# Attention and a mixture-of-experts layer on one core: values kept unsplit in DRAM and split by GpSimd head by head

## The chip, the core and the metric

The kernel runs on one core of a Trainium2 chip. The metric is the device time in microseconds of one execution. The core's engines each follow their own instruction list and meet only at semaphores: TensorE (PE) multiplies, VectorE (DVE), ScalarE (ACT) and GpSimd (POOL) work element by element, SyncE (SP) issues most DMAs. Matrix products are written with fp32r operands. To keep accuracy, an operand is split into a rounded part ("hi") and the rest ("lo"), and products are made with both.

## The reference

```
xn  = layernorm(x)                                   # x: 2 x 1024 x 512
att = softmax(causal(Q K^T / sqrt(32))) V, times Wo  # 16 heads of 32, Q, K, V = xn Wq^T, xn Wk^T, xn Wv^T
ffn = sum over the 2 chosen of 8 experts of w_e * mlp_e(xn) + shared_mlp(xn)
out = x + att + ffn
```

The tokens number 2048, in 16 tiles of 128. There are 2 x 16 = 32 heads of a batch row ("heads" below), each with 1024 queries and keys.

## The kernel before, in words

The work goes through phases: `norm_phase`, `project_phase`, `attend_phase`, `out_phase` and `routed_phase`. Each is a block with one list of instructions per engine, and a phase ends when all its lists have ended.

**norm_phase** (from line 179). Per tile of 128 tokens it loads x, normalizes it, turns it with four transposes, splits the turned tile into `tile_hi` and `tile_lo`, and multiplies by `wv` with twelve products into `ps_v`: that is V. The helper `pipeline(eng, count, unroll, stages, back)` writes each engine's list: at step s it calls, in the order given, each stage (lag, f) for tile s-lag. Four slots are used in turn. The lists are:

- SyncE: `load` (lag 0; line 235; waits until the x slot is normalized), `store_zeros` (0), `store_xn` (3; line 240), `store_v` (5; line 245).
- VectorE: `invert` (1; line 287), `statistics` (0; line 270), `scale` (1; line 294), `lo` (2; line 303), `mean_and_variance` (0; line 276), `split_wv` (2), `v_lo` (4; line 316), `add_eps` (0; line 281), `save_lo` (2; line 309).
- ScalarE: `root` (0; line 348), `hi` (1; line 356), `split_wv` (1), `save_hi` (1; line 361), `v_hi` (3; line 368).
- TensorE: `transpose` (0; line 385), then `multiply` (1; line 396).

V is split here. ScalarE's `v_hi` copies `ps_v` into the first half of each head's 64 columns of `v_stage`, and VectorE's `v_lo` writes `ps_v` less that into the second half. `store_v` waits for `v_lo_ready` and stores 128 x 16 x 64 floats, 512 KB, to `v_dram`. SyncE's list runs in a loop in the middle (`back=0`), the others too.

**project_phase** computes Q and K, the router's logits and the routing. SyncE's first loads there are the bias and a tile of `wqk` (line 476), which ScalarE splits first (line 526).

**attend_phase** (from line 743). One list of steps is written out for all engines: 32 heads of NB = 12 blocks, one block (a stretch of up to 512 queries by 128 keys) a step. Each stage has a lag: the row maxima run 24 steps (`AHEAD`) ahead of the scores (line 1433), exp (line 1213) has lag 24, `hi` 25 (line 1220), `lo` 26, the products with V `VALUE` = 30 (lines 1456 and 1458). `lo` (prob_lo, the rest of the probabilities) is made by GpSimd (line 1175) for ten blocks of a head and by VectorE for n = 4 and 8 (line 1302). The widths of a head's blocks n = 0 to 11 are 512, 256, 384, 128, 512, 256, 512, 384, 512, 128, 512 and 512. There are 4 buffers of `prob`, so exp of step s waits for the `lo` of step s-4. A fixed number of the shared MLP's products (lines 1489 and 1514) is put into each step of TensorE by `fill_counts`, from costs written in the code.

GpSimd's list has one `lo` per step and, after it, one step of `placing_steps`, the routing: 48 of them ahead of step 0, the last 32 being indirect DMAs to `slots_dram` (line 1145).

VectorE's `normalize` and `weigh_o` (lines 1327 and 1331) finish half a head's output. TensorE's `turn_row` (line 1420), once per head, waits for the L1331 of the half before.

SyncE's list goes by heads g: `load_head(g)` (six DMAs, lines 958 and 960, which wait until the scores of head g-4 are done), at certain g `load_xt`, `store_acc` and `load_base`, then `load_values(g - 1)` (line 967), then raw shared weights. `load_values` fetches 128 x 8 x 64 floats, 256 KB, in pieces of 256 bytes, into `vs`, which has four slots (`HS`) and is read directly as the stationary operand of the V products; it waits until head g-4 has been multiplied (`pv_done`). The last two columns of a slot are ones.

## Time and profile before

| | |
|---|---|
| median of 3 runs | 1165.86 us (1165.05 to 1168.9) |
| the profiled execution, its own time | 1170.92 us |
| its span, first to last instruction | 1169.1 us |
| mean granted TensorE clock | 0.963 of full speed |
| TensorE, VectorE, ScalarE, GpSimd busy | 1055.6, 769.1, 647.0, 505.2 us |
| norm_phase | about 0 to 70.8 us |
| project_phase | to about 183 us |
| attend_phase | to about 780 us |
| out_phase and routed_phase | the rest |

A row of a group gives the line, the engine, the operation, the tile written and the tile read, the shape and the count, then the busy time and the mean of one in ns, then the idle time of the engine just ahead of them and what ended it. A row of a timeline gives the start and the duration in us first; instructions of one kind that follow one another are merged into one row with their count. "SPq" and "ACTq" are the sequencers that issue DMAs.

### The profile page before, as it was taken

How to read it: one execution, taken by the hardware profiler on the slowest of the kernel's cores; microseconds unless marked ns; L12 is line 12 of the kernel's file. 1: busy time of each engine (PE TensorE's matmuls, PEld its weight loads, DVE VectorE, ACT ScalarE, POOL GpSimd, SP SyncE). 2: the span in 40 equal slices, each digit the busy share in tenths (PEclk: the TensorE clock that was granted, in tenths of full speed). 3: DMA queues.
4: the chain of work that ended last, by engine and by line, in shares of the span. 5: the costliest groups of instructions: out<-in, count | busy, mean ns of one | idle time of the engine just before them, and what ended most of it. 6: DMA issues, size and time to landing. Idle time of an engine off the chain costs nothing. (4 is left out here: it accounts for less than half of the span.)

```text
span 1169.1 us, 19196 instructions
## 1 busy us (share of the span) xinstructions
PE 1055.6 (90%) x5379; PEld 819.2 (70%) x5380; DVE 769.1 (66%) x1729; ACT 647.0 (55%) x1291; POOL 505.2 (43%) x566
## 2 busy tenths in 40 slices
PE   5979995978999999999999999989879999999994
PEld 4857873756677776777777777757668777777773
DVE  6832344646578878877777777555367777777782
ACT  4523220445677777777787777851155555555551
POOL 0001815389656555555655565540013333334331
PEclk9989996989899999999999999989989999999998
DMA  5987978578145265444343444038793334433332
GB/s 190 316 320 294 153 268 264 107 119 152 37 145 145 53 202 99 146 115 146 100 112 116 145 133 130 2 119 284 234 370 64 66 72 72 72 65 66 71 69 36
DMA packets 109559, 165.68 MB, mean 142 GB/s; under 512 B 54016, under 2 KB 64512, under 8 KB 106272
## 3 DMA queue, kind: packets, MB, share of 16 engines
q1 hardware_dynamic: 99136, 143.92, 43.0%
q0 software_dynamic: 9760, 20.49, 9.9%
q8 instruction: 37, 0.61, 0.2%
q14 instruction: 50, 0.41, 0.1%
q10 hardware_dynamic: 576, 0.26, 0.1%
HBM read 103.35 MB, written 61.28 MB: 141 GB/s over the span
## 5 line engine op out<-in xcount | busy, mean ns | idle before, releaser
L1175 POOL TENSOR_TENSOR prob_lo<-prob,prob_hi 128x512 fp32r<-128x512 f32 (+2 forms) x320 | 308.2, 977 | 224.2 <-ACT prob_hi L1220 169.4
L1213 ACT ACTIVATE prob<-ps_s 128x512 f32<-128x512 f32 (+3 forms) x384 | 188.2, 490 | 141.1 <-PE ps_s L1438 95.9
L1220 ACT ACTIVATE prob_hi<-prob 128x512 fp32r<-128x512 f32 (+3 forms) x384 | 198.5, 517 | 12.7 <-ACT row_stage L1194 12.7
L1283 DVE CUSTOM_DVE_ANT_0 ps_m<-ps_m,causal 128x384 f32<-128x384 f32 (+3 forms) x256 | 126.8, 496 | 75.2 <-PE ps_m L1409 74.1
L1851 DVE TENSOR_TENSOR rw_lo<-gu_sb,rw_hi 128x704 fp32r<-128x704 f32 x156 | 138.9, 893 | 48.9 <-ACT rw_hi L1786 44.3
L1765 POOL DMA_INDIRECT out<-work,rows x39 | 61.6, 1580 | 251.6 <-DVE rows L1812 131.5
L1409 PE MATMUL ps_m<-ks,qs 96*128 96x512 f32 (+3 forms) x384 | 140.0, 366 | 13.8 <-DMA ks<-qk_hi 12.8
L1786 ACT ACTIVATE rw_hi<-gu_sb 128x704 fp32r x156 | 123.4, 793 | 47.9 <-PE ps_ru L1884 32.4
L1433 PE MATMUL ps_s<-qs,ks 97*128 97x512 f32 (+3 forms) x384 | 138.3, 360 | 2.7 <-ACT prob L1213 2.6
L1456 PE MATMUL ps_o<-prob_hi,vs 128*66 128x512 f32 (+3 forms) x384 | 132.1, 344 | 9.3 <-issue 5.3
L1287 DVE TENSOR_REDUCE maxima<-ps_m 128x1 f32<-128x512 f32 x128 | 86.8, 686 | 69.2 <-PE ps_m L1409 68.8
L1458 PE MATMUL ps_o<-prob_lo,vs 128*66 128x512 f32 (+3 forms) x384 | 130.7, 341 | 0.0
L1905 PE MATMUL ps_ry<-d_sb,work 128*128 (+1 forms) x234 | 106.9, 592 | 1.2 <-issue 1.2
L1409 PEld LDWEIGHTS ps_m<-ks,qs 96*128 96x128 f32 x384 | 75.0, 196 | 36.6 <-issue 13.6
L1433 PEld LDWEIGHTS ps_s<-qs,ks 97*128 97x128 f32 x384 | 73.9, 193 | 18.4 <-ACT prob L1213 4.6
L1489 PE MATMUL ps_f<-xt,sg_hi 128*128 128x512 f32 (+1 forms) x192 | 73.0, 414 | 4.6 <-DMA xt<-xt_blocks 4.6
L1456 PEld LDWEIGHTS ps_o<-prob_hi,vs 128*66 128x66 f32 x384 | 53.6, 140 | 29.2 <-issue 13.8
L1777 ACT ACTIVATE xg_hi<-ps_xt 128x512 fp32r<-128x512 f32 x39 | 23.3, 598 | 91.3 <-PE ps_xt L1872 91.3
L1905 PEld LDWEIGHTS ps_ry<-d_sb,work 128*128 128x128 f32 (+1 forms) x234 | 43.1, 189 | 38.8 <-issue 38.8
L1489 PE MATMUL ps_f<-xt,su_hi 128*128 128x512 f32 (+1 forms) x192 | 70.3, 400 | 0.0
L1438 PE MATMUL ps_s<-late,eye 128*128 128x128 f32 x256 | 61.0, 238 | 0.0
L689 DVE TENSOR_TENSOR work<-ps_q,work 128x512 fp32r<-128x512 f32 x32 | 21.8, 690 | 58.8 <-ACT work L537 56.8
(211 smaller groups left out, 2416.2 us busy)
## 6 DMA issues: line engine op xcount, KB each, us to landing
xt<-xt_blocks SPq DMA_DIRECT2D x8, 2048.0 KB, 8.5
v_rows<-work SPq DMA_DIRECT2D x16, 512.0 KB, 2.9
qk_hi<-work SPq DMA_DIRECT2D x8, 1024.0 KB, 4.1
qk_lo<-work SPq DMA_DIRECT2D x8, 1024.0 KB, 7.0
qs<-qk_hi SPq DMA_DIRECT2D x64, 128.0 KB, 2.9
ks<-qk_hi SPq DMA_DIRECT2D x64, 128.0 KB, 3.1
vs<-v_rows SPq DMA_DIRECT2D x32, 256.0 KB, 5.0
out<-y_acc SPq DMA_DIRECT2D x32, 256.0 KB, 3.5
```

What stands on the lines that cost most here:

```text
L1175: nc.gpsimd.tensor_tensor(prob_lo[:, s % NPL, 0:w], prob[:, s % NP, 0:w], prob_hi[:, s % NPH, 0:w].bitcast(F32), ALU.subtract).then_inc(lo ...
L1213: nc.scalar.activation(prob[:, s % NP, 0:w], ps_s[s % NS][:, 0:w], ACT.Exp, scale=SCALE).then_inc(exp_done, 1)
L1220: nc.scalar.activation(prob_hi[:, s % NPH, 0:w], prob[:, s % NP, 0:w], ACT.Copy).then_inc(hi_ready, 1)
L1283: nc.vector.tensor_tensor_reduce(ps_m[s % NM][:, 0:w], ps_m[s % NM][:, 0:w], causal[:, TBW - w:], 1.0, MASKED, ALU.add, ALU.max, maxima[:, ...
L1409: nc.tensor.matmul(ps_m[s % NM][:, 0:w], qs[0:ROWS, c, t * P:(t + 1) * P], ks[0:ROWS, c, k0:k0 + w], start=True, stop=True).then_inc(m_don ...
L1433: last = nc.tensor.matmul(ps_s[s % NS][:, 0:w], ks[0:ROWS + 1, c, kt * P:(kt + 1) * P], qs[0:ROWS + 1, c, q0:q0 + w], start=True, stop=not ...
L1456: nc.tensor.matmul(into, vs[:, c, kt, :], prob_hi[:, s % NPH, 0:w], start=n in STARTS, stop=False)
L1458: nc.tensor.matmul(into, vs[:, c, kt, :], prob_lo[:, s % NPL, 0:w], start=False, stop=n in ENDS).then_inc(pv_done, 1)
L1489: last = nc.tensor.matmul(ps_f[part][0:w, :], (w_hi, w_lo, w_hi)[term][:, kc, f0:f0 + w], xt[:, (0, 0, 1)[term], kc, :], start=(j == 0), s ...
L1786: nc.scalar.activation(w_hi[:, k, :], chunk(e, k), ACT.Copy).then_inc(w_hi_ready, 1)
L1851: nc.vector.tensor_tensor(w_lo[:, k, :], chunk(e, k), w_hi[:, k, :].bitcast(F32), ALU.subtract).then_inc(w_lo_ready, 1)
L1905: last = nc.tensor.matmul(ps_y[c % 2][:, :], hid_t[0:w, c % HR, k, :], d_sb[0:w, bass.ds(e * NF + k, 1), :].rearrange("p a d -> p (a d)"), ...
```

## The change

V is stored whole: `v_dram` has 32 columns per head, ScalarE copies `ps_v` in one piece, `v_lo` on VectorE is gone, and `store_v` (now 256 KB, lag 4, all steps of SyncE written out) waits for ScalarE. In `attend_phase`, `load_values` goes to one buffer `v_raw` (128 KB in pieces of 128 bytes) two heads behind `load_head` instead of one, and waits until the head before has been split. GpSimd's list gets `split_values` behind `lo`, at the step at which a head's scores begin and the next one: a copy of 128 x 256 into the hi columns of `vs`, then a subtraction of 128 x 256 into the lo columns. TensorE waits for `values_split` instead of the load.

```diff
@@ -87,7 +87,7 @@
...
     qk_lo = nc.dram_tensor("qk_lo", [2 * D, T], F32, kind="Internal").ap()
-    v_dram = nc.dram_tensor("v_rows", [P, NT, H, 2 * DK], F32, kind="Internal").ap()
+    v_dram = nc.dram_tensor("v_rows", [P, NT, H, DK], F32, kind="Internal").ap()
     row_dram = nc.dram_tensor("max_rows", [2 * H, S], F32, kind="Internal").ap()
...
@@ -188,7 +188,7 @@
...
         rstd = sbuf("rstd", [P, U])
-        v_rows = U * H * 2 * DK // D
+        v_rows = U * H * DK // D
         xn = work[:, v_rows:v_rows + U, :]
...
@@ -197,8 +197,7 @@
...
         wv_lo = sbuf("wv_lo", [P, KC, D], F32R)
-        v_stage = work[:, 0:v_rows, :].bitcast(F32R).rearrange(
-            "p (u a) (h d) -> p u (a h) d", u=U, d=2 * DK)
+        v_stage = work[:, 0:v_rows, :]
         ps_t = [psum(f"ps_t{n}", [P, KC, P]) for n in range(U)]
...
@@ -220,8 +219,7 @@
...
         r_loaded = sem("r_loaded")
-        v_hi_ready = sem("v_hi_ready")
-        v_lo_ready = sem("v_lo_ready")
+        v_ready = sem("v_ready")
         zeros_ready = sem("zeros_ready")
...
@@ -241,9 +239,9 @@
...
                     t = U * i + c
-                    wait(sp, v_lo_ready, t + 1)
-                    sp.dma_start(v_dram[:, bass.ds(t, 1)].rearrange("p a h d -> p (a h) d"),
-                                 v_stage[:, c].bitcast(F32)).then_inc(v_stored[c], 16)
+                    wait(sp, v_ready, t + 1)
+                    sp.dma_start(v_dram[:, bass.ds(t, 1)].rearrange("p a h d -> p (a h d)"),
+                                 v_stage[:, c, :]).then_inc(v_stored[c], 16)
...
@@ -253,7 +251,8 @@
...
-                pipeline(sp, NT, U, [(0, load), (0, store_zeros), (3, store_xn), (5, store_v)])
+                pipeline(sp, NT, U, [(0, load), (0, store_zeros), (3, store_xn), (4, store_v)],
+                         back=NT)
...
@@ -309,14 +308,6 @@
...
-                def v_lo(i, c):
-                    t = U * i + c
-                    wait(dve, v_hi_ready, t + 1)
-                    v = v_stage[:, c]
-                    nc.vector.tensor_tensor(v[:, :, DK:], ps_v[c][:, :].rearrange("p (h d) -> p h d", h=H),
-                                            v[:, :, 0:DK].bitcast(F32),
-                                            ALU.subtract).then_inc(v_lo_ready, 1)
-
                 nc.vector.memset(zeros, 0.0).then_inc(zeros_ready, 1)
...
@@ -327,7 +318,7 @@
...
                     (1, invert), (0, statistics), (1, scale), (2, lo), (0, mean_and_variance),
-                    (2, split_wv), (4, v_lo), (0, add_eps), (2, save_lo)], back=U)
+                    (2, split_wv), (0, add_eps), (2, save_lo)], back=U)
...
@@ -361,15 +352,13 @@
...
-                def v_hi(i, c):
+                def save_v(i, c):
                     t = U * i + c
...
                     wait(act, v_stored[c], 16 * i)
-                    nc.scalar.activation(v_stage[:, c, :, 0:DK],
-                                         ps_v[c][:, :].rearrange("p (h d) -> p h d", h=H),
-                                         ACT.Copy).then_inc(v_hi_ready, 1)
-
-                pipeline(act, NT, U, [(0, root), (1, hi), (1, split_wv), (1, save_hi), (3, v_hi)])
+                    nc.scalar.activation(v_stage[:, c, :], ps_v[c][:, :], ACT.Copy).then_inc(v_ready, 1)
+
+                pipeline(act, NT, U, [(0, root), (1, hi), (1, split_wv), (1, save_hi), (3, save_v)])
                 act.wait_ge(r_loaded, 16)
...
@@ -389,7 +378,7 @@
...
                     wait(pe, lo_ready, t + 1)
-                    wait(pe, v_lo_ready, t - U + 1)
+                    wait(pe, v_ready, t - U + 1)
                     n = 0
...
@@ -844,6 +833,7 @@
...
         ks = sbuf("ks", [P, HS, S], F32R)
+        v_raw = sbuf("v_raw", [P, QT, DK])
         vs = sbuf("vs", [P, HS, QT, VW], F32R)
...
@@ -892,7 +882,8 @@
...
         head_loaded = [sem(f"head_loaded{n}") for n in range(HS)]
-        values_loaded = [sem(f"values_loaded{n}") for n in range(HS)]
+        values_loaded = sem("values_loaded")
+        values_split = sem("values_split")
         row_saved = sem("row_saved")
...
@@ -962,10 +953,10 @@
...
                 def load_values(g):
-                    c, h, b = g % HS, g // B, g % B
-                    wait(sp, pv_done, NB * (g - HS + 1))
-                    sp.dma_start(vs[:, c, :, 0:2 * DK].bitcast(F32),
-                                 v_dram[:, b * QT:(b + 1) * QT, h, :]).then_inc(values_loaded[c], 16)
+                    h, b = g // B, g % B
+                    wait(sp, values_split, 2 * g)
+                    sp.dma_start(v_raw[:, :, :], v_dram[:, b * QT:(b + 1) * QT, h]
+                                 ).then_inc(values_loaded, 16)
...
@@ -1017,8 +1008,8 @@
...
                             load_base(unit)
-                    if 0 < g <= HEADS:
-                        load_values(g - 1)
+                    if 2 <= g < HEADS + 2:
+                        load_values(g - 2)
                     for k in range(NF):
...
@@ -1177,9 +1168,22 @@
...
+                def split_values(s):
+                    g, c = s // NB, s // NB % HS
+                    if s % NB == 0:
+                        pool.wait_ge(values_loaded, 16 * (g + 1))
+                        wait(pool, pv_done, NB * (g - HS + 1))
+                        nc.gpsimd.tensor_copy(vs[:, c, :, 0:DK], v_raw[:, :, :]
+                                              ).then_inc(values_split, 1)
+                    if s % NB == 1:
+                        pool.wait_ge(values_split, 2 * g + 1)
+                        nc.gpsimd.tensor_tensor(vs[:, c, :, DK:2 * DK], v_raw[:, :, :],
+                                                vs[:, c, :, 0:DK].bitcast(F32),
+                                                ALU.subtract).then_inc(values_split, 1)
+
                 for _ in range(48):
                     next(placing_steps, None)
-                steps([(LO, lo)])
+                steps([(LO, lo), (AHEAD, split_values)])
                 for _ in placing_steps:
...
@@ -1445,7 +1449,7 @@
...
                     if n == 0:
-                        pe.wait_ge(values_loaded[c], 16 * (g // HS + 1))
+                        pe.wait_ge(values_split, 2 * (g + 1))
                     if n in STARTS:
...
```

## Rows read from the trace of the kernel before

**Rows 1.** The page, busy time, share of the span and instructions of an engine.

```profile
PE 1055.6 (90%) x5379; PEld 819.2 (70%) x5380; DVE 769.1 (66%) x1729; ACT 647.0 (55%) x1291; POOL 505.2 (43%) x566
```

**Rows 2.** Busy time of the engines by stretch, then clock, DMA share and GB/s.

```profile
240.00:273.00 33.00, 25.04 (x114) 19.18 (x114) 16.99 (x42) 15.59 (x37) 29.72 (x30) 0.84 0.78 152
...
306.00:339.00 33.00, 31.81 (x181) 25.02 (x180) 25.22 (x72) 25.86 (x58) 18.95 (x20) 1.00 0.46 129
```

**Rows 3.** Timeline of norm_phase, tiles 4 to 6 and 14.

```profile
26.40 0.60 PE L385 MATMUL ps_t<-ident,work 128*128 128x128 f32 x4
...
27.17 0.60 ACT L356 ACTIVATE tile_hi<-ps_t 128x512 fp32r<-128x512 f32 x1 [0.49 <-PE ps_t L385]
...
28.43 0.58 ACT L368 ACTIVATE work<-ps_v 128x512 fp32r<-128x512 f32 x1
...
30.44 0.69 DVE L270 BATCH_NORM_STATS2 stats<-x_tile 128x6 f32<-128x512 f32 x1 [0.21 <-DMA x_tile<-in_x]
...
31.05 0.53 DVE L294 TENSOR_SCALAR work<-x_tile,moments,rstd 128x512 f32<-128x512 f32 x1
...
32.87 0.14 DVE L281 TENSOR_SCALAR var_eps<-moments 128x1 f32<-128x1 f32 x1
...
58.95 0.60 PE L385 MATMUL ps_t<-ident,work 128*128 128x128 f32 x4
```

**Rows 4.** Timeline of the end of norm_phase, VectorE.

```profile
69.02 0.69 DVE L316 TENSOR_TENSOR work<-ps_v,work 128x512 fp32r<-128x512 f32 x1 [2.08 <-ACT work L368]
```

**Rows 5.** Waits from 222 to 300 us, and GpSimd's timeline at 295 us.

```profile
ACT prob L1213 <- POOL prob_lo L1175: 21.1, 18, 1.7
...
295.36 0.99 POOL L1145 DMA_INDIRECT slots<-entry,slot_of  x1 [0.17 <-issue]
```

**Rows 6.** TensorE's L1420 and VectorE's L1331, then timelines of two heads.

```profile
  DVE work L1331: 20.9, 28
...
L1331 DVE TENSOR_TENSOR work<-o_sum,o_inv x64: 291/338/1694, 239.3 to 779.8; 128x128 f32<-128x128 f32 x64
...
407.64 4.51 POOL L1175 TENSOR_TENSOR prob_lo<-prob,prob_hi 128x512 fp32r<-128x512 f32 x4 [1.03 <-ACT prob_hi L1220]
...
410.95 0.61 DVE L1331 TENSOR_TENSOR work<-o_sum,o_inv 128x128 f32<-128x128 f32 x1
...
676.56 1.29 POOL L1175 TENSOR_TENSOR prob_lo<-prob,prob_hi 128x512 fp32r<-128x512 f32 x1 [1.03 <-ACT prob_hi L1220]
...
678.08 3.51 POOL L1175 TENSOR_TENSOR prob_lo<-prob,prob_hi 128x512 fp32r<-128x512 f32 x3 [0.24 <-ACT prob_hi L1220]
...
680.16 0.84 DVE L1331 TENSOR_TENSOR work<-o_sum,o_inv 128x128 f32<-128x128 f32 x1
```

**Rows 7.** Timeline of SyncE's issues in norm_phase.

```profile
23.07 0.33 SPq L245 DMA_DIRECT2D v_rows<-work  x1
...
23.45 0.43 SPq L235 DMA_DIRECT2D x_tile<-in_x  x1
```

**Rows 8.** DMA issues near 23 and 16 us, then x loads' landings.

```profile
v_rows<-work SPq DMA_DIRECT2D x1, 512.0 KB, 2.9
...
x_tile<-in_x SPq DMA_DIRECT2D x1, 256.0 KB, 3.4
...
xn_rows<-work SPq DMA_DIRECT2D x1, 256.0 KB, 2.0
...
DMA to landing us min/median/max: 2.7/3.5/8.1
```

**Rows 9.** Groups of GpSimd by form.

```profile
L1175 POOL TENSOR_TENSOR prob_lo<-prob,prob_hi 128x256 fp32r<-128x256 f32 x64 | 48.2, 753 | 61.4 <-ACT prob_hi L1220 57.6 <-PE ps_o L1458 3.7
...
L662 POOL CAST sg_hi<-sg_raw 128x1408 fp32r<-128x1408 f32 x1 | 1.4, 1372 | 0.0
...
L669 POOL CAST sd_hi<-sd_raw 128x1024 fp32r<-128x1024 f32 x1 | 1.1, 1052 | 0.0
```

**Rows 10.** The page's DMA issues: count, KB each, median us to landing.

```profile
vs<-v_rows SPq DMA_DIRECT2D x32, 256.0 KB, 5.0
```

## The prediction

> **What bounds the kernel now.** I read the page first. TensorE is busy for 90% of the span [rows 1], so it is the engine to watch, but the mean hides three stretches that the change touches, and each has its own limit. The busy time by stretch shows two of them: from 306 us on TensorE is busy for 31.8 of 33 us while GpSimd has 19.0, but from 240 to 273 us GpSimd is busy for 29.7 of 33 us and TensorE for only 25.0 [rows 2].
>
> The first stretch, norm_phase, needs the timelines. TensorE's transposes start at 26.40 us for tile 4 and at 58.95 us for tile 14 [rows 3]: 32.55 us for ten tiles, 3.26 each. Inside it TensorE is busy throughout, so VectorE's `v_lo` (0.69 us, 16 times [rows 4]) lies beside it. What nearly ends last is a loop through SyncE: a load of x is queued behind a store of V, and the store waits until V is copied out.
>
> The end of the phase is a plain chain: ScalarE's copy, VectorE's `v_lo`, the last issue, the block's end, then the first w_raw load of the next phase. `v_lo` of tile 15, at 69.02 us, is the last of VectorE's work there [rows 4].
>
> In attention, ScalarE's exp waits 21.1 us in all for GpSimd's prob_lo between 222 and 300 us, and the last of the 32 routing DMAs on GpSimd starts at 295.36 us [rows 5]. Until then GpSimd sets the pace, afterwards TensorE does. In the later part TensorE stops once per head at `turn_row`, for L1331 on VectorE: 20.9 us over 28 heads [rows 6].
>
> **Norm phase: the SyncE queue.** `store_v` moves from lag 5 to lag 4. Before, the load of tile s+1 stood behind the store of V tile s-5; now it stands behind that of s-4. The first load that met a V store was that of tile 6 (store at 23.07, load at 23.45 us) [rows 7]. Now it is that of tile 5. V tile 0 is copied out one `v_lo` before its store, at 23.07-0.69 = 22.38 us at the latest; one issue (23.45-23.07 = 0.38 us) later load 5 goes, at 22.73 us.
>
> Call L the time from a load's issue to its landing. Statistics of tile 5 start at 22.73+L. From statistics to the end of scale there are 31.05+0.53-30.44 = 1.14 us [rows 3], and with an estimated 0.13 us of signalling the transpose starts 1.27 us after statistics. Tile 4's transpose is then at 24.00+L, against 26.40: a shift of L-2.40.
>
> The loop after that: the `root` of the next tile stands ahead of ScalarE's `hi`. VectorE reaches add_eps 32.87-30.44 = 2.43 us after statistics; without `v_lo` in front of it, about 0.6 us sooner. Root and signalling add an estimated 0.4, so `hi` starts at 2.2 us; V's copy ends 28.43+0.58-27.17 = 1.84 us after `hi` starts [rows 3]; store and next load take 0.41. So 4.45+L us after statistics of tile k+1 those of tile k+3 can start: two tiles in 4.45+L against 6.51 before. Over tiles 4 to 14 that is five times L-2.06. Together the phase grows by 6L-12.7.
>
> L is the large unknown. With a 512 KB store just ahead it was 3.4 us; that store alone landed in 2.9, a lone 256 KB store in 2.0, the quickest load of x in 2.7 [rows 8]. Taking the stores' slope (0.9 us for 256 KB) off 3.4 gives 2.5, the lower bound; the upper is 3.1, 2.7 for a load plus what is left of the smaller store. I take 2.75, since the quickest load is the nearest row. The phase then grows by 6 x 2.75 - 12.7 = **+3.8 us** (2.3 to 5.9).
>
> The Trainium skill (DMA: Bandwidth & Descriptors, Anatomy of one DMA) gives about 2.0 us fixed plus the bytes at 436 GB/s. For 512 KB of V and x behind one another that is an estimate of 3.2 us from the store's issue, L = 2.8, and the phase would grow by 4.1 us by it. Our own lone store of 2.0 us is already quicker than its 2.6.
>
> **The phase's end.** The last `v_lo` (0.69 us) was on the path [rows 4]: **-0.7 us**. The first w_raw load stood behind a 512 KB store and now behind 256 KB; between nothing and the 0.9 us that separates the two stores [rows 8], I take **-0.4 us**. The router's r_lo moves up with it. ScalarE's copy keeps its 512 elements: nothing. Unrolling SyncE's loop saves only sequencing on a queue that mostly waits: nothing beyond what L covers.
>
> **Attention: two more GpSimd instructions per head.** The subtraction of 256 elements is the form 128x256 of prob_lo, 0.753 us. The copy goes by the two CASTs, 1.372 us for 1408 elements and 1.052 for 1024: slope 0.83 ns, so 0.41 us for 256 [rows 9]. Consecutive GpSimd instructions overlap by about 0.05 us (four of them, 512, 512, 512 and 256 wide, take 4.51 us [rows 6]), so a head adds 0.36+0.70+0.04 of waits = 1.1 us. No row shows the copy's strided write; it could cost nothing or half as much again.
>
> Head 0's split comes before the first prob_lo, where GpSimd idles: nothing. Those of heads 1, 2 and 3 fall between 240 and 296 us, where GpSimd sets the pace: 3 x 1.1 = **+3.3 us** (2.0 if waits elsewhere swallow one, 4.8 if strides cost). TensorE does not win it back, because its filling work is fixed per step.
>
> The other 28 splits fall between prob_lo of n = 10 and 11 and between 11 and 0. ScalarE's exp four steps on needs these; its margin is about one us, so the delay is hidden. If that cover goes, each head costs up to 1.1 us.
>
> But the order on GpSimd also sets when L1331 is let through. VectorE's L1331 is ready at 410.95, takes 0.61 us where the quickest takes 0.29, and ends just after GpSimd's third 512 (407.64 + 3 x 1.26 = 411.4); TensorE goes on at once [rows 6]. Afterwards GpSimd's instruction boundaries lie at 1.26, 1.6, 2.9, 3.65 and 4.9 us from the group's start instead of 1.26, 2.5, 3.8. L1331, ready at 3.31, is let through at 3.65 instead of 3.8. In some later heads ScalarE delays the second 512 (678.08 us in the group of 676.56 us): L1331, ready at 3.60, ends only at 4.4 [rows 6]. There the copy fills the gap and some 0.3 is won. 28 x 0.1 is 2.8 us. The bounds are -5 and, with slow strides, +3; I take **-2.5 us**.
>
> Value loads halve in bytes and come a head later. SyncE now waits in `load_values` for the split of the head before, some 4 us per head; behind it stand only raw weights that are needed much later and the next `load_head`, which waits longer anyway. A value load landed in a median of 5.0 us [rows 10], and has about twelve steps of 1.4 us, less those 4: hidden.
>
> **Sum:** 3.8-0.7-0.4+3.3-2.5 = +3.5 us. The profiled execution took 1170.92 us (span 1169.1 and 1.8 around it), 5.1 above the median of 1165.86. Added to its own time that is 1174.4; against the median, 1169.4. I give the latter.
>
> **Rivals.**
> - *No loop in norm_phase.* If L drops to 2.1, like the lone store, the phase stays at TensorE's pace: +3.5-3.8 gives about -0.3 us, 1165.6. For: the traffic per tile falls by a quarter. Against: no x load landed in under 2.7.
> - *L1331 slips in a boundary earlier* (the faster side). After the change a boundary lies near 2.9 us from the group's start. L1331 is ready at 3.1 (the least of the 28 heads) to 3.6. If copy and waits take 0.2 to 0.4 us longer than I think, the boundary reaches it in over half of the heads and TensorE's stop of about 0.6 us is gone there: 18 x 0.6 = 10.8 us off; with the other terms (+6) it ends at about 1161. It decides at a boundary later than 3.1 us. The Trainium skill (SBUF — State Buffer, Who interferes with whom) says that a VectorE instruction with two SBUF inputs and a GpSimd instruction that reads SBUF exclude each other for the whole instruction, whoever starts first; by it any boundary serves, and the trace agrees (0.61 against 0.29 us).
> - *L1331 slips past the subtraction.* If it becomes ready after 3.65 us, it waits for the third 512 until 4.9: +1.1 us a head, for ten heads 11 us: 1180. Its readiness reached 3.6, so this is close.
> - *A value load late.* If a base load ahead of it delays one past its split, GpSimd stops for one to three us in a few heads: 1172 to 1175.
>
> **Chances.** Forecast 0.45, no loop 0.2, L1331 earlier 0.15, L1331 later 0.12, late values 0.08. A measurement of this kernel tells about 0.3% (3.5 us) from no change. My forecast lies on that edge, so half of its chance is "same"; the no-loop case is "same"; both late cases are "slower"; L1331 earlier is "faster". Faster 0.16, same 0.41, slower 0.43. The forecast's own bounds, all low or all high, are -2 and +13 (1164 to 1179); with the earlier L1331 taken in and the rarest of the late ends left out the range is 1161 to 1178.
>
> **What would show it.** Transposes in norm_phase 3.5 to 3.7 us apart with short TensorE gaps, waiting on VectorE and x; the first projection product some 3 us later than before; two GpSimd rows of about 0.4 and 0.75 us, 32 times each; the last routing DMA about 6 us later; the stop at `turn_row` slightly under 0.75 us a head. I am wrong if the transposes stay 3.26 us apart, or if turn_row's stop in total moves by more than 5 us.

## The result, and the profile after

The changed kernel is slower: 1180.8 us in the median of 15 runs (1170.37 to 1185.67) against 1162.55 us for 15 runs of the kernel before (1154.81 to 1168.9). The ratio of the means is 1.0132, 95% interval 1.0104 to 1.0161, or 15.4 us (12.1 to 18.7); the medians lie 18.3 us apart. The forecast was 1169.4, its range ended at 1178, and the least likely rival but one (chance 0.12) had said 1180. All of these were counted from 1165.86 us, the median of three runs; as differences the forecast was +3.5 us and the end of its range +12. The profiled execution took 1183.31 us with a span of 1180.7.

The table places the difference by milestones of TensorE, each number a mean of three profiled executions of one kernel, in us (lines are those of before; after's are in brackets).

| stretch on TensorE | before | after | difference |
|---|---|---|---|
| start to the first product of projection, L577 (L566) | 76.0 | 80.4 | +4.4 |
| from there to the first product of attention, L1409 (L1413) | 117.1 | 121.0 | +3.9 |
| to `turn_row` of head 0, L1420 (L1424) | 14.4 | 13.6 | -0.7 |
| `turn_row` of head 0 to that of head 5 | 104.5 | 106.5 | +2.0 |
| head 5 to head 15 | 168.0 | 165.2 | -2.8 |
| head 15 to head 24 | 149.9 | 158.9 | +9.05 |
| head 24 to the last product of attention | 147.7 | 146.0 | -1.6 |
| from there to the end of the span | 388.7 | 387.3 | -1.4 |

Five terms matter: the norm phase, the projection phase, the first heads, and two of opposite sign in the heads that follow. Of these, +9.05 repeats to 0.1 us in all three profiles; +3.9 does not (117.9, 121.7 and 123.4 us after, 116.9 to 117.4 before). The -1.4 is no effect that could be told from chance: the same stretch differs by 3.5 us among the three profiles of before. The whole table adds up to 12.8 us, the difference of the mean spans.

The page's line of busy time:

```profile
PE 1060.9 (90%) x5379; PEld 820.4 (69%) x5380; DVE 762.7 (65%) x1713; ACT 647.8 (55%) x1291; POOL 537.8 (46%) x630
```

Busy time by stretch, columns as in [rows 2], the second stretch holding the ends of heads 16 and 17:

```profile
240.00:273.00 33.00, 27.04 (x138) 20.82 (x137) 19.73 (x53) 16.92 (x39) 29.60 (x31) 0.90 0.75 107
...
500.00:533.00 33.00, 29.37 (x167) 22.92 (x167) 26.77 (x65) 24.46 (x55) 20.26 (x23) 1.00 0.44 120
```

Against [rows 1], GpSimd has 32.6 us and 64 instructions more, VectorE 6.4 us and 16 fewer. From 240 to 273 us GpSimd is as full as in [rows 2]. From 500 to 533 us it has room for 12 us, and yet TensorE is busy 2.4 us less than in the steady stretch of before.

What the split costs stands in the groups of GpSimd by form:

```profile
L1180 POOL TENSOR_TENSOR vs<-v_raw,vs 128x256 fp32r<-128x256 f32 x32 | 23.0, 720 | 0.2
L1176 POOL CAST vs<-v_raw 128x256 fp32r<-128x256 f32 x32 | 14.4, 450 | 4.8 <-DMA v_raw<-v_rows 4.7
```

In the steady heads the two take 0.69 and 0.40 us; the means hold a few that ran beside VectorE. The estimate had 0.753 and 0.41. All of the idle time is one wait, before the first head: value loads are on time.

Norm phase, two of the longest waits up to 72 us (what waits for what: us, times, longest):

```profile
DVE stats L269 <- DMA x_tile<-in_x: 18.7, 12, 3.3
PE ps_t L374 <- DVE work L293: 11.2, 8, 6.5
```

Timelines of the same phase, the transposes of tiles 4 and 14 and two of SyncE's issues:

```profile
25.68 0.54 PE L374 MATMUL ps_t<-ident,work 128*128 128x128 f32 x3 [0.59 <-DVE work L293]
...
63.83 0.65 PE L374 MATMUL ps_t<-ident,work 128*128 128x128 f32 x4
...
24.21 0.32 SPq L243 DMA_DIRECT2D v_rows<-work  x1
24.57 0.43 SPq L233 DMA_DIRECT2D x_tile<-in_x  x1
```

Ten tiles take 38.15 us instead of the 32.55 of [rows 3], and VectorE waits 18.7 us for x in all, three times the 6.0 us of before. The load of x is issued right after the store of V that it stands behind, 0.36 us later: the loop through SyncE is there.

Now the steady heads. VectorE's product `work<-o_sum,o_inv`, L1331 in [rows 6], is L1335 here. The timelines of GpSimd, VectorE and TensorE at the end of head 16, the first of the nine long ones:

```profile
501.55 1.29 POOL L1166 TENSOR_TENSOR prob_lo<-prob,prob_hi 128x512 fp32r<-128x512 f32 x1 [1.07 <-ACT prob_hi L1224]
502.79 0.40 POOL L1176 CAST vs<-v_raw 128x256 fp32r<-128x256 f32 x1
503.15 1.29 POOL L1166 TENSOR_TENSOR prob_lo<-prob,prob_hi 128x512 fp32r<-128x512 f32 x1
504.40 0.69 POOL L1180 TENSOR_TENSOR vs<-v_raw,vs 128x256 fp32r<-128x256 f32 x1
505.06 1.25 POOL L1166 TENSOR_TENSOR prob_lo<-prob,prob_hi 128x512 fp32r<-128x512 f32 x1
...
505.16 1.30 DVE L1335 TENSOR_TENSOR work<-o_sum,o_inv 128x128 f32<-128x128 f32 x1
...
506.61 0.27 PE L1424 MATMUL ps_x<-ident,maxima 128*8 128x128 f32 x1 [1.57 <-DVE work L1335]
```

GpSimd's group starts at 501.55. Its next instructions start 1.24, 1.60, 2.85 and 3.51 us later. L1335 becomes ready 3.61 us after the start, 0.10 us after the subtraction has given way to the third 512, and takes 1.30 us, to just past the end of that instruction. TensorE stands for 1.57 us. In heads 5 to 15 L1335 is ready while the subtraction still runs, takes 0.36 to 0.40 us in eight of the eleven heads and about 0.6 in three, and TensorE stands for 0.14 to 0.39 us instead of about 0.6 before. That is the -2.8 and -1.6 of the table, and the nine long heads (16 to 24, stops of 1.35 to 2.05 us) are the +9.05.

What ended TensorE's idle time before L1424, to be set beside the first row of [rows 6]:

```profile
  DVE work L1335: 22.3, 25
```

The sum hides the matter: 22.3 us after 20.9, since short stops got shorter and nine got long. Only the stops head by head show it.

### The profile page after: what moved, and what is told of

It reads as the page before. It is cut to its first block and busy times, and to the rows that moved or that the text cites. A ratio compares the mean times of both kernels' runs of the same rounds, so it can differ in the third digit from the quotient of the medians.

```text
span 1180.7 us, 19201 instructions
## 1 busy us (share of the span) xinstructions
PE 1060.9 (90%) x5379; PEld 820.4 (69%) x5380; DVE 762.7 (65%) x1713; ACT 647.8 (55%) x1291; POOL 537.8 (46%) x630
## 5 line engine op out<-in xcount | busy, mean ns | idle before, releaser
L1413 PE MATMUL ps_m<-ks,qs 96*128 96x512 f32 (+3 forms) x384 | 140.6, 368 | 13.7 <-DMA ks<-qk_hi 12.8
L1790 ACT ACTIVATE rw_hi<-gu_sb 128x704 fp32r x156 | 123.5, 793 | 48.7 <-PE ps_ru L1888 33.8
L1413 PEld LDWEIGHTS ps_m<-ks,qs 96*128 96x128 f32 x384 | 75.2, 196 | 36.7 <-issue 13.7
L1437 PEld LDWEIGHTS ps_s<-qs,ks 97*128 97x128 f32 x384 | 74.2, 193 | 26.4 <-ACT prob L1217 10.4
L1460 PEld LDWEIGHTS ps_o<-prob_hi,vs 128*66 128x66 f32 x384 | 53.9, 140 | 28.2 <-issue 14.6
L566 PE MATMUL ps_q<-xt_hi,w_hi 128*128 128x512 f32 x128 | 52.0, 406 | 12.1 <-DVE w_lo L668 6.6
```

What stands on the lines that cost most here:

```text
L1413: nc.tensor.matmul(ps_m[s % NM][:, 0:w], qs[0:ROWS, c, t * P:(t + 1) * P], ks[0:ROWS, c, k0:k0 + w], start=True, stop=True).then_inc(m_don ...
L1437: last = nc.tensor.matmul(ps_s[s % NS][:, 0:w], ks[0:ROWS + 1, c, kt * P:(kt + 1) * P], qs[0:ROWS + 1, c, q0:q0 + w], start=True, stop=not ...
L1460: nc.tensor.matmul(into, vs[:, c, kt, :], prob_hi[:, s % NPH, 0:w], start=n in STARTS, stop=False)
L1790: nc.scalar.activation(w_hi[:, k, :], chunk(e, k), ACT.Copy).then_inc(w_hi_ready, 1)
```

## The experiments

Times are set against the kernel before on the same chip. "Stretch" is the time from the first product of projection to the first of attention.

| kernel | ratio to before, 95% interval | first projection product | stretch | heads 0 to 5 | heads 15 to 24 |
|---|---|---|---|---|---|
| a1_lag5 | 1.0096 (1.0059 to 1.0133) | 73.81 | 121.2 | 106.3 | 158.9 |
| a2_late_split | 1.0073 (1.0043 to 1.0103) | 80.26 | 120.3 | 106.6 | 149.9 |
| a3_norm_only | 1.0072 (1.0048 to 1.0097) | 79.68 | 123.3 | 104.0 | 149.8 |
| a4_attn_only | 1.0043 (1.0022 to 1.0064) | 75.66 | 117.6 | 106.7 | 159.0 |
| b3_lag5_late | 1.0003 (0.9975 to 1.0031) | 73.96 | 123.1 | 106.6 | 149.9 |
| b4_longer | 1.0088 (1.0055 to 1.0121) | 80.15 | 123.1 | 107.0 | 149.4 |
| c1_same_place | 1.0019 (0.9995 to 1.0042) | 72.56 | 118.0 | 105.7 | 149.9 |
| c2_looped | 1.0007 (0.9987 to 1.0027) | 75.02 | 115.7 | 106.7 | 149.9 |
| c3_spread | 1.0019 (0.9995 to 1.0042) | 73.02 | 120.8 | 95.3 | 149.9 |
| c4_pads_act | 1.0011 (0.9989 to 1.0034) | 74.29 | 116.7 | 106.7 | 149.9 |
| d1_same_place | 1.0093 (1.0057 to 1.0129) | 78.61 | 117.8 | 106.0 | 159.0 |
| d3_after_again | 1.0107 (1.0059 to 1.0154) | 79.86 | 117.9 | 106.8 | 159.0 |
| d4_slots | 0.9909 (0.9878 to 0.9941) | 73.25 | 122.7 | 89.2 | 149.8 |
| e1_before_slots | 0.9879 (0.9841 to 0.9917) | 76.19 | 116.9 | 89.4 | 149.9 |
| e2_four_slots | 1.0104 (1.0050 to 1.0158) | 73.45 | 123.5 | 97.5 | 149.9 |

**One part at a time.** a1_lag5, from the changed kernel:

```diff
-pipeline(sp, NT, U, [(0, load), (0, store_zeros), (3, store_xn), (4, store_v)],
+pipeline(sp, NT, U, [(0, load), (0, store_zeros), (3, store_xn), (5, store_v)],
          back=NT)
```

> The changed kernel with `store_v` back at lag 5 in SyncE's order of norm_phase; V is still stored whole, 256 KB a tile. Theory (the queue loop costs the norm phase its 3.5 us): load s+1 again stands behind the store of tile s-5, the transposes of tiles 4 to 14 are again 3.2 to 3.3 us apart instead of 3.8, and the first projection product starts at 75 to 76.5 us instead of 79.99. Attention keeps its shape: about nine heads with a stop of 1.3 to 2.1 us at turn_row. Time 3.5 to 4.5 us under the changed kernel, ratio to before about 1.010. Rival (the norm phase is slower for another reason, such as what the smaller stores do to the DMA traffic): the transposes stay 3.8 us apart and the product near 80 us.

The first projection product came at 73.81 us, 6 us earlier than in the changed kernel and 2 us earlier than before: lag 4 is the whole loss of the norm phase, whose transposes are 3.2 us apart again. What makes it quicker than before (the missing `v_lo`, the smaller stores, SyncE's list written out) was not separated. VectorE's wait for x fell from 18.7 us to 3.7. The nine heads stayed.

a2_late_split, from the changed kernel:

```diff
 def split_values(s):
...
-    if s % NB == 0:
+    if s % NB == 2:
...
-    if s % NB == 1:
+    if s % NB == 3:
...
```

> The changed kernel with GpSimd's split moved by two steps: the copy comes after prob_lo of n = 0 and the subtraction after that of n = 1, so that around `weigh_o` (the product that VectorE does before turn_row) GpSimd's instruction boundaries are again those of before. The amount of work is the same. Theory (a late `weigh_o` slips past the subtraction): the stops at turn_row of 1.3 to 2.1 us in heads 16 to 24 go back to 0.6 to 0.9, the stretch from turn_row of head 15 to that of head 24 takes about 150 us instead of 159, time 8 to 10 us under the changed kernel, at or below before's plus 3. Rival A (GpSimd simply has too much work, 1.1 us a head more): the stretch stays at 155 us or more wherever the split stands. Rival B (the longer stretch comes from later value loads or another wait): the same.

The theory held to 0.1 us: heads 15 to 24 take 149.9 us. At head 16 GpSimd runs both 512s in one piece, and L1335, ready 3.61 us after the start of the group as in the changed kernel, takes 0.33 us:

```profile
502.75 2.53 POOL L1166 TENSOR_TENSOR prob_lo<-prob,prob_hi 128x512 fp32r<-128x512 f32 x2
...
505.10 0.33 DVE L1335 TENSOR_TENSOR work<-o_sum,o_inv 128x128 f32<-128x128 f32 x1
```

The amount of work is the same, so rival A falls; so does B. The size was expected too large (8 to 10 us under the changed kernel, at most 3 over before): 8.5 us are left over before, 7 fewer than the changed kernel's 15.4. With the nine long stops the gain of the other heads went too (about 0.6 us of stop again in each), and the long stretch stayed.

a3_norm_only and a4_attn_only exchange the two halves, each with the edits of the diff in one phase alone. Both leave out the lower part of V in the products: a3 loads whole values straight into the first half of `vs` and sets the second half to zero, a4 splits values that have no lower part left.

> The norm phase of the changed kernel (V stored whole, lag 4) with the attention of before: no split on GpSimd, the value load goes straight into the place that the products read, and only into its first half, in pieces of 128 bytes; the second half is set to zero once. It leaves out the lower part of V in the products; the number and shapes of the products are kept. Theory: norm phase as in the changed kernel (first projection product at 79 to 80.5 us, +3.5), attention as before (turn_row to turn_row of heads 15 to 24 about 150 us, no stop above 1 us, GpSimd-paced heads 1 to 3 without the extra 2.4 us); ratio to before 1.003. If the extra 6 us between the first projection product and the first attention product belong to the change, they are seen here again; if they are chance of the transfers, they are seen in some of these kernels and not in others. Rival (the norm phase's delay shifts what comes later and so makes the slow heads): stops of 1.3 us or more in heads 16 to 24 here too, ratio 1.010 or more.

> The norm phase of before (V split there, stores of 512 KB, lag 5) with the attention of the changed kernel: GpSimd splits a head's values, loaded from the first halves alone. It leaves out the lower part of V, which comes out as zero; all instructions of the attention are there. Theory: first projection product at 76 to 77 us as before; attention as in the changed kernel, with some nine heads of 1.3 to 2.1 us at turn_row, +2.4 us in heads 1 to 3; ratio to before 1.006 to 1.010. With a3_norm_only the two excesses should add up to that of the changed kernel (1.013). Rival (the slow heads need the norm phase's delay as well): no stop above 1 us, ratio under 1.004.

Both theories held in where the time goes, the nine long stops in a4 alone, but neither ratio was met: a3 came to 1.0072 instead of 1.003, a4 to 1.0043 instead of 1.006 to 1.010. The excesses, 0.72 and 0.43%, add up to 1.15%, inside the interval of the changed kernel. Of a3's 8 us only 3 to 4 come from the norm phase; its profiled execution had a stretch of 123.3 us, 6 more than before, which the prediction had not priced. In a4, with split stores, the stretch stayed at 117.6.

**More work, less time.** b4_longer, from the changed kernel:

```diff
+spare = sbuf("spare", [P, 2, DK])
...
 nc.gpsimd.tensor_copy(vs[:, c, :, 0:DK], v_raw[:, :, :]
                       ).then_inc(values_split, 1)
+nc.gpsimd.tensor_copy(spare[:, :, :], v_raw[:, 0:2, :])
```

> The changed kernel with more work: GpSimd copies another 128x128 elements to a place that nobody reads, right after its copy of the split, some 0.3 us a head. Theory (`weigh_o` misses the end of the subtraction by 0.1 us and is then shut out for a whole 512 instruction): the subtraction now ends 0.3 us later, `weigh_o` becomes ready inside it in all heads, the nine long stops of 1.4 to 2.1 us shrink to 0.5 to 0.8, the others grow from 0.37 to about 0.65; heads 15 to 24 take about 151 us instead of 159 and the kernel gets 2 to 6 us faster by doing more, although heads 1 to 3, which GpSimd paces, lose 1 us. Rival (GpSimd has too much work per head, or the stops come from something else): nothing is gained, and each head is 0.3 us longer or the same; time 0 to 10 us above the changed kernel.

The size given there is a slip: the copy is 128x64. Head 16 again:

```profile
502.53 1.30 POOL L1167 TENSOR_TENSOR prob_lo<-prob,prob_hi 128x512 fp32r<-128x512 f32 x1 [1.07 <-ACT prob_hi L1226]
503.78 0.40 POOL L1177 CAST vs<-v_raw 128x256 fp32r<-128x256 f32 x1
504.12 0.23 POOL L1179 COPY spare<-v_raw 128x64 f32<-128x64 f32 x1
504.32 1.29 POOL L1167 TENSOR_TENSOR prob_lo<-prob,prob_hi 128x512 fp32r<-128x512 f32 x1
505.56 0.69 POOL L1182 TENSOR_TENSOR vs<-v_raw,vs 128x256 fp32r<-128x256 f32 x1
...
506.15 0.29 DVE L1337 TENSOR_TENSOR work<-o_sum,o_inv 128x128 f32<-128x128 f32 x1
```

The product is ready 3.62 us after the group's start, the same as in the changed kernel, but the subtraction now ends at 3.72, so that the product is let in as soon as it ends and takes 0.29 us. Eight of the nine long stops are gone (head 19, ready later, keeps 2.22 us); heads 15 to 24 take 149.4 us instead of 158.9. GpSimd does 0.2 us a head more, and yet from its first to its last product attention takes 583.6 us against 589.4 to 591.0 in the three profiles of the changed kernel. In the whole time the gain is within the intervals: 1.0088 beside 1.0132 and 1.0107 of the changed kernel.

**The two repairs together**, b3_lag5_late (both diffs above):

> The changed kernel with both repairs: `store_v` back at lag 5 and the split two steps later on GpSimd. Theory (the two costs are separate and add up): first projection product at 74 us (2.5 us before that of before), attention as in a2_late_split (no stop above 1.2 us, heads 1 to 3 still 2.4 us longer in all); ratio to before 0.998 to 1.004. Rival (they are not separate, or the smaller stores cost elsewhere, between projection and attention): 1.006 or more.

The time is that of before, 1.0003. Its profiled execution, the slowest of its twelve runs, shows the long stretch all the same (123.1), so that stretch may vary from run to run.

**The stretch in the projection phase.** Repeats, and two possible causes:

> The changed kernel once more, unchanged: how much of its profile repeats? The nine heads with a stop of 1.3 to 2.1 us (heads 16 to 24) are set by the order of instructions and should be there again, the stretch of heads 15 to 24 at 159 us again, and the transposes of norm_phase about 3.8 us apart again. Left open by the first four runs: the 3 to 6 us between the first projection product and the first attention product (123.4 us in the changed kernel, 117.4 in before). Theory (it comes with the whole stores of V): 120 us or more again. Rival (chance of the transfers): 117 to 119 us here.

> The kernel before once more, unchanged, for the same question: from the first projection product to the first attention product 117 to 118 us if that stretch is fixed by the kernel, 119 to 123 us here if it is chance. Stops at turn_row again 0.6 to 1.2 us in every head, 20.9 us in all; first projection product at 76 us.

They gave 121.7 and 116.9 us. In the phase ScalarE waits for the seventh load of w_raw, which stands on SyncE's queue behind the store of the routing table's pads, 39 KB in pieces of 8 bytes. That wait in the timeline of before, and then in that of the changed kernel:

```profile
156.79 0.63 ACT L526 ACTIVATE w_hi<-w_raw 128x512 fp32r<-128x512 f32 x1 [10.15 <-DMA w_raw<-in_wqk]
```

```profile
163.71 0.63 ACT L515 ACTIVATE w_hi<-w_raw 128x512 fp32r<-128x512 f32 x1 [14.55 <-DMA w_raw<-in_wqk]
```

The pads in the changed kernel's DMA issues (KB, us from issue to landing; 23.3 before):

```profile
slots<-slot_table SPq DMA_DIRECT2D x1, 39.0 KB, 27.3
```

In the ten profiles with a long stretch (120 us or more) ScalarE waited 12.0 to 14.6 us for this load, in the ten others 9.4 to 11.6. TensorE runs dry in the wait, and its granted clock from 150 to 180 us was 0.89 to 0.94 in the ten long ones and 1.00 in the others. So a longer wait is paid twice.

c1_same_place (from b3_lag5_late) and d1_same_place (from the changed kernel):

```diff
-v_dram = nc.dram_tensor("v_rows", [P, NT, H, DK], F32, kind="Internal").ap()
+v_dram = nc.dram_tensor("v_rows", [2, P, NT, H, DK], F32, kind="Internal").ap()[0]
```

> b3_lag5_late (V stored whole, lag 5, late split), with the tensor of V in HBM declared as large as before and only its first half used, so that every tensor behind it, the slot table's among them, is at the address that it had before. What is open: from the first projection product to the first attention product it took 116.9 to 117.6 us in the three profiles with split stores of V and 120.3 to 123.4 us in the seven with whole ones, and the store of the pads to the slot table took 23.3 to 24.0 against 24.9 to 27.3 us. Theory (the address of the slot table decides how fast its 4992 small writes go): pads in 23 to 24 us, the stretch back at 117 to 118 us. Rival (it comes from the order or the size of DMAs in norm_phase): 120 us or more again, pads 25 us or more.

c2_looped is b3_lag5_late without `back=NT`, so that SyncE's list runs in its loop again:

> b3_lag5_late with SyncE's order of norm_phase in its loop again instead of written out in full (`back=NT` taken away). Theory (addresses): nothing changes, the stretch from the first projection product to the first attention product stays at 120 to 123.5 us. Rival (the unrolled issues of the norm phase leave the queue in another state for the small writes that follow): back at 117 to 118 us. The norm phase itself: transposes 3.2 to 3.3 us apart as in b3_lag5_late, first projection product within 0.5 us of 74.

118.0 and 115.7 us: each met the number of the theory or rival that the other refutes, so this pair decides nothing. On the next chip:

> The changed kernel with the tensor of V declared as large as before and its first half used, so that the addresses of the tensors behind it are those of before; nothing else differs from d3_after_again, on the same chip. Theory (the address of the slot table makes its small writes slower): from the first projection product to the first attention product 117 to 118.5 us here and 120 to 123.5 in d3_after_again; time 4 us less. Rival (timing left behind by the norm phase at lag 4): 120 us or more in both, times within 2 us.

> The changed kernel once more, on the same chip as d1_same_place and timed with it. From the first projection product to the first attention product 120 to 123.5 us by both theories, the nine locked heads again; ratio to before about 1.013.

> The kernel before once more, beside the other two on the same chip. From the first projection product to the first attention product 116.5 to 118 us by both theories; 119 or more would say that chance alone can lengthen this stretch.

117.8, 117.9 and 116.9 us. The changed kernel itself can have the short stretch, and d4_slots and e2_four_slots, with the old addresses, had 122.7 and 123.5: the address theory falls. What remains is a count, over several chips. With split stores of V all five profiles had 116.9 to 117.6 us; with whole ones ten of fifteen had 120.3 to 123.5, the rest 115.7 to 118.0. The cause stays open, chance included.

**The pads from another queue.** c4_pads_act moves `store_pads` from SyncE's order to ScalarE's, at the same step, in b3_lag5_late:

> b3_lag5_late with the store of the pads (39 KB in pieces of 8 bytes) issued from ScalarE's queue instead of SyncE's, at the same step. Theory (the load of w_raw waits 10 to 14 us because it stands behind these pieces in one queue, and TensorE's clock falls in the stop that follows): the wait for w_raw falls under 3 us, TensorE does not stop, and the stretch from the first projection product to the first attention product takes 110 to 115 us instead of 123; 5 to 12 us faster than b3_lag5_late. Rival (the small pieces fill the 16 DMA engines whatever queue they come from): the wait stays at 8 us or more, time unchanged.

ScalarE still waited 10.3 us for w_raw. The small pieces hold up the load from either queue. While they run, the engines are busy and move nearly nothing (a window of the kernel before, columns as in [rows 2]; the DMA share is above 1 where the times of packets overlap):

```profile
135.00:140.00 5.00, 5.00 (x24) 4.14 (x23) 2.59 (x3) 1.72 (x3) 4.85 (x4) 1.00 1.93 2
```

**The first heads.** c3_spread adds two empty steps after each routing DMA in b3_lag5_late:

```diff
...
     entry[:, t, k, :], None).then_inc(entries_stored, 16)
 yield
+yield
+yield
...
```

> b3_lag5_late with the 32 routing DMAs of GpSimd spread over every third step of attention instead of every step. Theory (heads 1 to 5 are paced by GpSimd alone, at 17 to 28 us a head against 16.6 later, and the split's 2.4 us are lost there): heads 1 to 5 come down to under 20 us each, the split costs nothing more there, and the kernel is 8 to 20 us faster than b3_lag5_late, so faster than before. Rival (these heads are paced by VectorE or by late loads of xt, GpSimd only looks busy): turn_row of head 5 no more than 3 us earlier. A DMA standing between prob_lo steps in more heads can shut `weigh_o` out there: one or two stops above 1.3 us are possible.

Heads 0 to 5 took 95.3 us instead of 106.6, but TensorE stood 2.1 to 3.4 us at `turn_row` in heads 2 to 9, and at head 9 nothing was left of it. A DMA now stood between the 512s, and the product waited through it, through the next 512 and through the copy of the split behind that. Head 6:

```profile
317.47 0.99 POOL L1136 DMA_INDIRECT slots<-entry,slot_of  x1
318.49 1.27 POOL L1168 TENSOR_TENSOR prob_lo<-prob,prob_hi 128x512 fp32r<-128x512 f32 x1
319.69 0.41 POOL L1178 CAST vs<-v_raw 128x256 fp32r<-128x256 f32 x1
...
317.85 2.40 DVE L1337 TENSOR_TENSOR work<-o_sum,o_inv 128x128 f32<-128x128 f32 x1
```

The copy ends at 320.10 us and the product at 320.25. In head 9 it waited through the DMA and four instructions more, 3.64 us. Where the product became ready beside a `prob_lo` or a subtraction, as in the heads above, it was let in at the next boundary; why it was not after a DMA, no run shows.

So the DMAs were put into steps far from it. d4_slots, from c1_same_place, with a list `routing_now` that is empty until the DMAs begin:

```diff
+routing_now.append(1)
 for t in range(NT):
...
-next(placing_steps, None)
+if not routing_now or n in (4, 6, 8):
+    next(placing_steps, None)
```

> c1_same_place with the 32 routing DMAs of GpSimd placed only at the steps n = 4, 6 and 8 of a head (three a head), far from the steps in which VectorE's product for turn_row is made. Theory (heads 1 to 5 are paced by GpSimd's total of work, and c3_spread's stops of 2.2 us came from a DMA between prob_lo of n = 10 and 0, which moved GpSimd's boundaries): heads 2 to 10 take 16.5 to 18 us each without stops above 1.2 us, turn_row of head 10 comes 15 to 20 us earlier than in c1_same_place (391.61 there), and the kernel is 10 to 20 us faster than before, ratio about 0.985. Rival (something else, such as the late first load of xt or the fill given to those steps, holds heads 1 to 5): head 10 no more than 5 us earlier.

It beats both kernels: 1156.08 us, ratio 0.9909. Heads 0 to 5 take 89.2 us, head 10 comes 12 us earlier after head 0 than in c1 (15 to 20 were expected); two heads of 20 us are left (2 and 10), and ahead of the second a value load came 4.6 us late. The same placing without the change, and four DMAs a head:

> The kernel before with one edit: the 32 routing DMAs of GpSimd only at the steps n = 4, 6 and 8 of a head, as in d4_slots; V split in norm_phase as before. Theory (the split costs what it adds to a GpSimd that has no room, and nothing once it has): head 10 as early after head 0 as in d4_slots within 2 us (155.4 us there from turn_row of head 0 to that of head 9), time within 3 us of d4_slots, 10 us under before. Rival (the split costs 2.4 us in heads 1 to 3 whatever else stands there): 3 to 6 us under d4_slots.

> d4_slots with four DMAs a head, at n = 4, 5, 7 and 8. Theory (three a head leave GpSimd time to spare, and the twelfth head's waits come from the DMAs ending late): they end three heads earlier and the two long heads around head 10 (20.3 us) come down to 17, 2 to 4 us faster than d4_slots. Rival (four a head fill GpSimd: 9.4 us of prob_lo, 1.1 of the split and 4.6 of DMAs in 16.3 us): heads 2 to 9 grow to 18 us or more, and it is slower than d4_slots by 5 us or more.

e1 (that edit alone in the kernel before) took 1153.49 us, 0.9879; head 9 comes 155.55 us after head 0 against 155.40 in d4: with room on GpSimd these two profiles show no cost of the split there, and the intervals of the two ratios overlap. e2 lost what d4 had won, 1.0104. Four a head make GpSimd the pace again, heads 2 to 9 take 19 to 22 us. Head 10, which was to come down from 20.3 us to 17, came down to 18.7.

## Why the prediction was wrong, by its steps

**Queue loop in norm_phase: right in mechanism, too small.** Predicted +3.8 us and transposes 3.5 to 3.7 us apart; ten tiles took 5.6 us more, 3.8 apart, where the prediction's period made it 3.5 us more. The term mis-sized is L, taken from the quickest load (2.75 us); the median landing in the changed kernel is 3.1, and the loop's period, 4.45+L for two tiles, gives L = 3.2 for the measured 7.63. The first term, a shift of tile 4's transpose by L-2.40 = 0.35 us, can't be tested: that transpose starts at 25.1 to 26.4 us in the three profiles of before and at 25.7 to 27.2 in those of after. At tile 14 the phase is 4.9 us late in the first pair of profiles and 5.9 in the means, inside the bounds of 2.3 to 5.9. The figure (2.0 us and 436 GB/s) that the prediction took from the Trainium skill (DMA: Bandwidth & Descriptors, Anatomy of one DMA) is a fit for DMAs that GpSimd issues; these are SyncE's. a1_lag5 showed that the lag alone does it. The end of the phase (-1.1) held: from tile 14's transpose to the first projection product it is 1.35 us shorter (17.51 to 16.16).

**Projection phase: not in the prediction.** +3.9 us in the mean of three. The pads were never looked at, although the wait of 10.15 us is in the trace of before. a3_norm_only, with the change in the norm phase alone, had it (123.3 us), but no run showed that the change causes it.

**First heads: right, a little large.** Predicted +3.3 us, measured +2.0 (+2.4 in the first pair of profiles); the last routing DMA starts at 306.95 us instead of 295.36 [rows 5], 2.1 us more than attention itself starts later.

**The term of -2.5 us for the order on GpSimd: this step failed.** It came out at +4.65 us. It said that L1331, "ready at 3.31, is let through at 3.65 instead of 3.8". Two numbers of it were wrong together. The subtraction gives way at 3.51 us, not 3.65: it starts at 2.85 instead of 2.9 and takes 0.69 us, with the overlap 0.66, instead of the 0.753 of prob_lo. And ready at 3.31 is true of one group of heads: in the trace of before L1331 is ready at 3.60 to 3.62 us (once 3.92) in heads 16 to 24, at 3.06 to 3.32 in heads 5 to 15. Heads 26 to 28 are at 3.60 too, but there ScalarE holds up the second 512 and with it the boundaries; the one head of 3.60 in [rows 6] is of that kind, and the text says "reached 3.6", without a count. With 0.05 us between 3.60 and 3.65 even the predicted boundaries left the sign of the term open for nine heads at once. The heads outside the nine gave -4.4 us, near the favourable bound of -5; the nine gave +9.05.

**The rival.** *L1331 slips past the subtraction* had the place, the price (1.1 us a head against 1.0) and the number of heads (ten against nine). Its stated point of decision, 3.65 us, was the faulty number. That its 1180 us met the measured median is in part luck: it held nothing for the projection phase (+3.9) and kept the -2.5 us, and it started from a median 3.3 us above that of the 15 runs. The Trainium skill (SBUF — State Buffer, Who interferes with whom) says that a VectorE instruction with two SBUF inputs contends with a GpSimd instruction that reads SBUF, and that the one issued later is blocked; the trace agrees, 1.30 us for L1335 beside a 512 of 1.25 that started 0.10 us ahead of it. b4_longer shows that the boundary decides: moved 0.2 us later it undid eight of nine.

**The test named for it was blunt.** It would be wrong "if turn_row's stop in total moves by more than 5 us": it moved by 1.4.

**Hidden parts.** Value loads and SyncE's new waits were hidden, as said: one wait of 4.7 us, before the first head.

**The sum.** The steps of attention and norm give 4.4+2.0-2.8+9.05-1.6 = 11.1 us, and the projection's 3.9 makes 15.0. With the two small stretches that no step explains (-0.7 and -1.4) the profiled executions differ by 12.8 us, near the lower end of the 12.1 to 18.7 measured over 15 runs each.

## What to carry to other kernels

Where two engines shut each other out of SBUF, what counts is at which instruction boundary the waiting one becomes ready, not how busy either is. List its readiness for every iteration against the boundaries as they will be; if one group lies within a tenth of a microsecond of a boundary, price both sides by their count. Put added work on such an engine where nobody waits for it, and look there first for work that already stands in the wrong place: the change with both repairs gave nothing (1.0003), and moving 32 DMAs gave 0.9 to 1.2%.

## What the runs showed of the hardware that was not expected

A GpSimd copy of 0.23 us that nobody reads brought eight stops of TensorE from 1.35 to 1.60 us down to 0.34 to 0.59. Where VectorE's product became ready during an indirect DMA of GpSimd (0.99 us), it was let in neither behind the DMA nor behind the 512 that followed, but 0.15 us after the end of the third instruction, and took 2.40 us. The 8-byte pieces of the pads (39 KB) landed after 22.5 to 27.4 us, kept the DMA engines busy at 2 GB/s, and held up a 256 KB load by 10 us also from another engine's queue.
